# Macaron block (routed FFN, retention, routed FFN) on one core: two head groups' attention outputs in shared PSUM rows, and a GpSimd product and subtraction rewritten

## The chip, the cores and the metric

The kernel runs on 1 of the 8 cores of a Trainium2 chip. The metric is the device time of one execution in microseconds (us), as the median of several runs; lower is better. Engines: PE (TensorE, matmuls and transposes), DVE (VectorE), ACT (ScalarE), POOL (GpSimd), SP (issues DMAs). Each engine works through its own list of instructions in order, and waits on semaphores where the list says so.

## The reference, cut to what matters

```
x = x + 0.5 * ffn(layernorm(x));  x = x + retention(layernorm(x));  x = x + 0.5 * ffn(layernorm(x))     # x: (16, 256, 128)

def ffn(src):                                        # 16 heads of 8 dims, 4 experts, d_ff 512
    q, k, v = (src @ Wn + bn, split into 16 heads)
    probs = softmax(q @ k.T * 8 ** -0.5)
    x = layer_norm(src + (probs @ v) @ Wo + bo) * ln1_g + ln1_b
    keys = x @ router_w + router_b                   # one number a token
    e = remainder(floor(keys), 4)                    # each token to one of four experts
    return layer_norm(x + relu(x @ W1[e] + b1[e]) @ W2[e] + b2[e]) * ln2_g + ln2_b
```

## The kernel before, in words

There are three parts in a row: a phase of attention and experts for all 16 batches of 256 tokens, retention, and a second phase like the first. In an attention phase the step `i` of a software pipeline handles several batches at once: scores of batch `i`, softmax weights times values of batch `i-1`, output projection and first layer norm of `i-2`, routing and sorting of `i-3`, and preparation (layer norm, transposition) of `i+1` and `i+2`. A step has eight slots, `p = 0..7`, one for each pair of heads. In each slot PE runs a burst of eight matmuls (lines 576 and 582: scores of two heads of `i`, and the scores shifted by their maximum of two other heads), DVE takes the row maxima of the burst's first half (line 1357) and ACT the exponential of the second (line 1047). There is one pair of PSUM banks for each, so a burst waits for the maximum and the exponential of the slot before. All other work is placed by hand between the bursts, and the order of each engine's list is the order in the code. Steps `base+4` to `base+13` of a phase are a hardware loop, the others are written out.

PSUM banks beside these: `pv_bank` for weights times values, and `bank_a`, `bank_b`, `bank_c`, which many small steps use in turn; `take(which, reader, value)` waits until the last reader of the bank has finished.

What the change touches, by line:

- Values. ACT copies `v` to `v_nat` (line 1025). POOL's `place_v` (line 1849) spreads eight heads at a time into `v_st`, 32 columns a head: 8 values, a one (for the sum of the weights), zeros.
- `weigh_values(b, g)` (PE, line 632) multiplies group `g` (four heads) of `v_st` with the weights. Four heads fill 4 x 32 rows of `pv_bank`; the groups 0 and 1 lie side by side in columns, and groups 2 and 3 overwrite them after ACT's `out_pv` (line 1055) has copied all 512 columns to `att_un`.
- `att_to_tokens` (PE, line 641, slot 6) transposes the four groups for both halves of the tokens, eight 128x128 transposes into two banks. `normalize` (DVE, lines 1366 and 1368, in slot 6 for one half, in slot 7 for the other) takes reciprocals of the sums and multiplies.
- POOL's `rstd` and `normalise` (lines 1826, 1828, 1835): variance plus epsilon, power of -0.5, then for each half of the tokens `(x - mean) * rstd`. It is done for `prep` of batch `i+2` and for `ln1` of batch `i-2`. The result of `prep`, `s_nat`, is what PE transposes in slot 2 of the next step (line 545).
- POOL in a step, in this order: `place_v(i, 0)`; `rstd`, `normalise`, `make_x1` (lines 1854, 1856) and `own_row` (line 1867) of `i-2`; `place_v(i, 1)`; `sort_out` of `i-3` with two indirect DMAs (line 1879); `rstd`, `normalise` and `add_bo` (line 1840) of `i+2`.
- DVE's `route(b, base, n)`: `n = 0` is the product of `x1` with the router's weights (line 1403), `n = 1` its sum (line 1406), the rest tiny steps down to the expert's mask. The first three stand in slot 0 of step `i`, for batch `i-3`. `place` (lines 1425, 1429, 1431) in slots 4 and 5 turns masks into row numbers and counts.

Of the kernel before, what the change touches and what calls it, by code (L numbers as in the profile page):

```python
# [61 lines left out]
VC = 32  # L62

# [25 lines left out]
def spread_heads(a):  # L89


    return np.ascontiguousarray(a.reshape(2, RH // 2, RK, -1).transpose(1, 0, 2, 3)).reshape(QK_DIM, -1)

# [38 lines left out]
def packed(A):  # L132

    A = dict(A)
    columns = A.pop("W_qkv").T
    A["W_qkv"] = np.concatenate([spread_heads(columns[0:QK_DIM]), spread_heads(columns[QK_DIM:2 * QK_DIM]), columns[2 * QK_DIM:]], 0).T
    A["w_att"] = np.concatenate([A.pop(n) for n in ("Wq", "Wk", "Wv", "Wo")], 1)
    A["bias_rows"] = np.concatenate([A.pop("b1").reshape(CHUNKS, P), A.pop("bq")[None], A.pop("bk")[None], A["bv"][None]], 0)
    A["vecs"] = np.concatenate([A.pop(n).reshape(-1) for n in ("bv", "bo", "ln1_g", "ln1_b", "ln2_g", "ln2_b", "router_w", "router_b")])
    return A  # L140
# [9 lines left out]
def build(nc, A):  # L150

    ctx = ExitStack()
    with ctx:
# [40 lines left out]
        eps_ln = sb("eps_ln", [P, TT])  # L194
        eps_gn = sb("eps_gn", [P, 16])
# [12 lines left out]
        v_nat = sb("v_nat", [P, TT, P])  # L208
        v_st = sb("v_st", [P, TT, NH, VC])
        att_un = sb("att_un", [P, GROUPS, SEQ])  # L210
        rsum = sb("rsum", [P, TT * GROUPS, GH])
# [102 lines left out]
        seed = {"ln2": sem("seed_ln2")}  # L314
        ln_sem = {"prep": prep_ln, "ln1": ln1, "ln2": ln2}
# [212 lines left out]
        def _(pe):  # L528
# [114 lines left out]

            def att_to_dims(b, base):

                pe.wait_ge(att_ready, b * 2 + 2)
# [116 lines left out]
            def phase(base):  # L763
# [4 lines left out]
                def body(i, part=range(PAIRS)):  # L768
                    if live(i - 2, base):
                        turn["a"], turn["b"] = (att_ready, (i - 2) * 2 + 2), (att_ready, (i - 2) * 2 + 1)  # L770
# [1260 lines left out]
```

## Time and profile before

| | |
|---|---|
| median of 3 runs | 948.08 us (946.7 to 950.37) |
| the profiled execution | 951.38 us, its span 949.3 us |
| busy: PE, DVE, ACT, POOL | 87%, 80%, 70%, 60% of the span |
| first attention phase, its experts' tail | to about 310 us, to about 400 us |
| retention | about 400 to 570 us |
| second attention phase, its experts' tail | to about 850 us, to the end |

Times in the rows below are microseconds from the start of the span. Durations in one execution of the hardware loop repeat from step to step within some hundredths of a microsecond, so one step stands for all.

### The profile page before, as it was taken

The numbers are of one execution on the slowest core, as the hardware profiler recorded it, in microseconds if no ns is written. First come the engines' busy times: TensorE is split into PE (matmuls) and PEld (weight loads), VectorE is DVE, ScalarE is ACT, GpSimd is POOL, SyncE is SP. The second block draws the span as 40 slices with busy tenths as digits, with TensorE's granted clock in tenths as the row PEclk, the third lists the DMA queues.
The fourth block names the chain that finished last, engine by engine and source line by source line (L and its number), as shares of the span: only waits on it lengthen the run. The fifth ranks groups of instructions, "written<-read, shape, count | busy, mean of one in ns | idle before, by whom it ended". The sixth has DMA issues, their size and how long they took to land.

```text
span 949.3 us, 26557 instructions
## 1 busy us (share of the span) xinstructions
PE 828.5 (87%) x8607; PEld 625.8 (66%) x8607; DVE 762.0 (80%) x1935; ACT 665.3 (70%) x1370; POOL 568.6 (60%) x801
## 2 busy tenths in 40 slices
PE   4899899999999688479999979999999999996883
PEld 3566666666666688457877856666666666666883
DVE  5688788888897877669898864888888888978775
ACT  2588788888887477435454554988888888874774
POOL 5135667576665667627777682265765757565666
PEclk9999999999999999889999995999999999998998
DMA  9995698000004667230000000000000000046671
GB/s 288 380 417 82 164 412 362 12 11 22 11 23 134 187 197 236 76 87 2 0 0 0 1 1 2 2 13 12 11 22 11 22 11 11 24 143 201 193 240 48
DMA packets 41812, 96.64 MB, mean 102 GB/s; under 512 B 5224, under 2 KB 25470, under 8 KB 37260
## 3 DMA queue, kind: packets, MB, share of 16 engines
q1 hardware_dynamic: 36236, 83.11, 27.1%
q0 software_dynamic: 5504, 12.63, 3.8%
q8 instruction: 37, 0.61, 0.2%
q14 instruction: 35, 0.29, 0.1%
HBM read 43.64 MB, written 53.13 MB: 102 GB/s over the span
## 4 chain that ended last, share of the span: by engine, by line
PE 45%; DVE 20%; issue 18%; POOL 13%; DVEq 1%; ACT 1%; DMA 1%; POOLq 0%; ACTq 0%
DVE mx L1357 9%; PE duo L576 8%; PE duo L632 7%; PE duo L569 3%; POOL out L1930 3%; DVE qk_lo L1346 2%; PE duo L882 2%; POOL x_mid L1930 2%; PE duo L641 2%; PE duo L861 2%; POOL xs L1922 2%; PE duo L570 2%; PE duo L870 2%; PE duo L723 2%; PE duo L840 2%
## 5 line engine op out<-in xcount | busy, mean ns | idle before, releaser
L1357 DVE TENSOR_REDUCE mx<-duo 128x4 fp32r<-128x1024 f32 x256 | 312.2, 1220 | 73.5 <-PE duo L576 68.4
L1047 ACT ACTIVATE probs<-duo 128x1024 f32<-128x1024 f32 x256 | 263.3, 1029 | 58.3 <-PE duo L582 53.7
L576 PE MATMUL duo<-stacks 32*128 32x256 f32 x1024 | 133.6, 338 | 36.3 <-DVE mx L1357 27.3
L632 PE MATMUL duo<-probs,v_st 128*32 128x256 f32 x2048 | 140.3, 392 | 0.3
L582 PE MATMUL duo<-q_st,stacks 32*128 32x256 f32 x1024 | 131.5, 335 | 0.1
L576 PEld LDWEIGHTS duo<-stacks 32*128 32x128 f32 x1024 | 80.7, 191 | 72.6 <-issue 32.7
L1826 POOL TENSOR_TENSOR a_ln<-mv_ln,eps_ln 128x2 f32<-128x2 f32 x32 | 6.3, 197 | 145.3 <-DVE mv_ln L1322 145.1
L569 PE MATMUL duo<-qk_hi,sel_r 128*128 128x256 f32 x256 | 83.0, 345 | 7.6 <-DVE qk_lo L1346 7.6
L632 PEld LDWEIGHTS duo<-probs,v_st 128*32 128x32 f32 x2048 | 54.1, 110 | 41.5 <-issue 3.4
L723 PE MATMUL duo<-w,xs 128*128 x608 | 77.0, 281 | 4.3 <-DVE hidden L1524 1.8
L582 PEld LDWEIGHTS duo<-q_st,stacks 32*128 32x128 f32 x1024 | 77.9, 188 | 1.4 <-ACT probs L1047 0.5
L1879 POOL DMA_INDIRECT x_sorted<-rows,pos_all x64 | 66.2, 1035 | 19.8 <-issue 19.8
L723 PEld LDWEIGHTS duo<-w,xs 128*128 128x128 f32 x608 | 73.4, 197 | 5.5 <-issue 5.5
L1039 ACT ACTIVATE q_st<-duo 128x256 fp32r<-128x256 f32 x128 | 50.5, 395 | 35.0 <-PE duo L616 26.2
L570 PE MATMUL duo<-qk_lo,sel_r 128*128 128x256 f32 x256 | 69.6, 292 | 0.0
L1078 ACT ACTIVATE xs<-duo,wside 128x256 f32<-128x256 f32 x152 | 59.8, 471 | 10.7 <-PE duo L709 10.3
L569 PEld LDWEIGHTS duo<-qk_hi,sel_r 128*128 128x128 f32 x256 | 50.6, 198 | 23.8 <-DVE qk_lo L1346 12.5
L1033 ACT ACTIVATE stacks<-duo,small 128x256 fp32r<-128x256 f32 x128 | 61.9, 484 | 0.0
L1669 DVE TENSOR_TENSOR ret<-duo,dm 128x768 f32<-128x768 f32 x64 | 58.0, 947 | 1.2 <-PE duo L864 1.2
L1849 POOL TENSOR_TENSOR v_st<-v_nat,ones_wide 128x128 f32<-128x128 f32 x64 | 29.4, 461 | 44.4 <-PE duo L632 44.0
L1032 ACT ACTIVATE stacks<-duo 128x256 fp32r<-128x256 f32 x128 | 49.3, 385 | 8.6 <-PE duo L570 8.2
L1835 POOL TENSOR_SCALAR s_nat<-xs,mv_prep,rstd_prep 128x128 f32<-128x128 f32 x64 | 50.6, 795 | 6.5 <-POOL rstd_prep L1828 6.4
(219 smaller groups left out, 2178.8 us busy)
## 6 DMA issues: line engine op xcount, KB each, us to landing
x_sorted<-ret SPq DMA_DIRECT2D x2, 17476.0 KB, 49.0
wbuf<-w_pack SPq DMA_DIRECT2D x38, 512.0 KB
ret<-x_sorted SPq DMA_DIRECT2D x22, 257.0 KB
stacks<-x_sorted SPq DMA_DIRECT2D x12, 257.0 KB
wside<-w_pack SPq DMA_DIRECT2D x38, 66.0 KB
w_pack<-wbuf SPq DMA_DIRECT2D x2, 1024.0 KB, 8.4
decay_rows<-prow SPq DMA_DIRECT2D x1, 1536.0 KB
xs<-x_sorted SPq DMA_DIRECT2D x4, 257.0 KB
```

Of the source, the lines that this page charges most:

```text
L569: pe.matmul(half, sel_r[:, g, 2 * n, :], qk_hi[:, n, :], start=True, stop=False)
L570: last = pe.matmul(half, sel_r[:, g, 2 * n + 1, :], qk_lo[:, n, :], start=False, stop=True)
L576: return pe.matmul(score_bank[h % 2][:, t * SEQ:(t + 1) * SEQ], q_st[r:r + 32, g, t * P:(t + 1) * P], k_st[r:r + 32, g, :], start=True, st ...
L582: return pe.matmul(banks[h % 2][:, t * SEQ:(t + 1) * SEQ], k_st[r:r + 32, g, t * P:(t + 1) * P], q2_st[r:r + 32, g, :], start=True, stop=True)
L632: last = pe.matmul(pv_bank[32 * j:32 * j + 32, cols], v_st[:, t, h, :], probs[:, h % RING, t, :], start=(t == 0), stop=(t == TT - 1))
L723: last = pe.matmul(sum_bank(k)[:, t * P:(t + 1) * P], hid[:, n % 2, c, t * P:(t + 1) * P], w2[:, bass.ds(e * CPE + c, 1), :], start=(c == ...
L1033: act.activation(k_st[:, g, :], o[:, SEQ:2 * SEQ], ACT.Identity, bias=ones_col[:]).then_inc(ex_ready, 1)
L1047: act.activation(probs[:, h % RING:h % RING + 2, :, :], duo_now[:].rearrange("p (n t q) -> p n t q", n=2, t=TT), ACT.Exp, scale=SCALE).the ...
L1078: act.activation(hid[:, n % 2, c, :], bank[c][:, 0:SEQ], ACT.Relu, bias=wside[:, n % 3, c:c + 1]).then_inc(h_ready, 1)
L1357: dve.tensor_reduce(rows, score_duo[:].rearrange("p (n t k) -> p n t k", n=2, t=TT), AX.X, ALU.max, negate=True).then_inc(max_done, 1)
L1669: dve.tensor_tensor(ret[:, 2 * g:2 * g + 2, :], both, dm[:, 2 * g:2 * g + 2, :], ALU.mult).then_inc(ret_ready, 1)
L1879: pool.indirect_dma_start(x_sorted[b // BATCH], bass.IndirectOffsetOnAxis(pos_all[:, b - base, t:t + 1], 0), rows[:, b - base, t, :], None ...
```

## The change

Values of two groups go into one block of columns with an offset of 16, so that the output of the first group of a half lands in rows 0 to 8 and that of the second in rows 16 to 24 of each 32 rows, and both accumulate into the same 256 columns of `pv_bank`. So there is one copy of 256 columns for each half, four transposes in place of eight, into one bank, and one `normalize` in place of two, in slot 7. `Wo` and `bv` are put into the matching order on the host. The number of matmuls of line 632 stays. On POOL, `rstd` also computes minus the mean (one more small instruction), and `normalise` adds it in place of subtracting the mean. The product of the routing goes from DVE (slot 0 of step `i`, for `i-3`) to POOL (between `make_x1` and `own_row` of step `i`, for `i-2`), for all batches but the last of a phase.

```diff
+PAIR = GH * VC + VC // 2
...
-        v_nat = sb("v_nat", [P, TT, P])
-        v_st = sb("v_st", [P, TT, NH, VC])
+        v_nat = sb("v_nat", [P, 2, TT, P // 2])
+        v_st = sb("v_st", [P, 2, TT, 2 * PAIR])
...
                 if g == 0:
                     pe.wait_ge(va_ready, b + 1)
-                    wait(pe, un_ready, b * 2)
+                    wait(pe, un_ready, b * 2 - 1)
                 if g == 2:
                     pe.wait_ge(vb_ready, b + 1)
-                    pe.wait_ge(un_ready, b * 2 + 1)
-                cols = slice((g % 2) * SEQ, (g % 2 + 1) * SEQ)
+                    wait(pe, un_ready, b * 2)
+                half, second = g // 2, g % 2
+                into = pv_bank[:, half * SEQ:(half + 1) * SEQ]
                 for t in range(TT):
                     for j in range(GH):
-                        h = g * GH + j
-                        last = pe.matmul(pv_bank[32 * j:32 * j + 32, cols], v_st[:, t, h, :], probs[:, h % RING, t, :],
-                                         start=(t == 0), stop=(t == TT - 1))
+                        first = P * second + VC * j
+                        last = pe.matmul(into[32 * j:32 * j + 32, :], v_st[:, half, t, first:first + VC], probs[:, (g * GH + j) % RING, t, :],
+                                         start=(t == 0 and not second), stop=(t == TT - 1 and second == 1), skip_group_check=True)
...
-            def att_to_tokens(b, t):
+            def att_to_tokens(b):
                 pe.wait_ge(un_ready, b * 2 + 2)
-                o = take("ba"[t], att_ready, b * 2 + t + 1)
-                for g in range(GROUPS):
-                    last = pe.transpose(o[:, g * P:(g + 1) * P], att_un[:, g, t * P:(t + 1) * P], ident[:])
+                o = take("b", att_ready, b + 1)
+                for t in range(TT):
+                    for half in range(2):
+                        last = pe.transpose(o[:, (2 * t + half) * P:(2 * t + half + 1) * P], att_un[:, half, t * P:(t + 1) * P], ident[:])
                 last.then_inc(att_ps, 1)
...
-                act.activation(att_un[:, 2 * half:2 * half + 2, :], pv_bank[:].rearrange("p (a q) -> p a q", a=2),
-                               ACT.Copy).then_inc(un_ready, 1)
+                act.activation(att_un[:, half, :], pv_bank[:, half * SEQ:(half + 1) * SEQ], ACT.Copy).then_inc(un_ready, 1)
...
-            def normalize(b, t):
-                dve.wait_ge(att_ps, b * 2 + t + 1)
+            def normalize(b):
+                dve.wait_ge(att_ps, b + 1)
                 wait(dve, attT_ps, b)
-                m = (bank_b, bank_a)[t][:].rearrange("p (n c) -> p n c", c=32)
+                m = bank_b[:].rearrange("p (n c) -> p n c", c=VC // 2)
...
                         if p == 0:
                             if live(i - 3, base):
-                                for n in range(3):
+                                for n in range(0 if is_last(i - 3, base) else 1, 3):
                                     route(i - 3, base, n)
...
                 pool.wait_ge(done, b * 8 + 4)
                 pool.tensor_tensor(s["a"][:], s["mv"][:, :, 1], eps_ln[:], ALU.add).then_inc(done, 1)
+                if steps == 1:
+                    pool.tensor_tensor(s["c"][:], s["mv"][:, :, 0], minus_one[:], ALU.mult).then_inc(neg_mean[which], 1)
                 pool.wait_ge(done, b * 8 + 5)
                 pool.tensor_tensor(s["rstd"][:], s["a"][:], half_root[:, 0:TT], ALU.pow).then_inc(done, steps)
...
                 pool.wait_ge(done, b * 8 + 6)
+                pool.wait_ge(neg_mean[which], nth)
                 for t in range(TT):
-                    pool.tensor_scalar(dst(t), src(t), s["mv"][:, t, 0:1], s["rstd"][:, t:t + 1], ALU.subtract, ALU.mult).then_inc(done, 1)
+                    pool.tensor_scalar(dst(t), src(t), s["c"][:, t:t + 1], s["rstd"][:, t:t + 1], ALU.add, ALU.mult).then_inc(done, 1)
...
-                src = v_nat[:, :, 64 * half:64 * half + 64].rearrange("p t (h d) -> p t h d", h=8)
-                pool.tensor_tensor(v_st[:, :, heads, 0:HD], src, ones_wide[:].unsqueeze(1).to_broadcast([P, TT, 8, HD]), ALU.mult).then_inc((va_ready, vb_ready)[half], 1)
+                src = v_nat[:, half, :, :].rearrange("p t (a j d) -> p (t a) j d", a=2, j=GH)
+                pool.tensor_tensor(v_place(half, slice(0, HD)), src, ones_wide[:, 0:GH, :].unsqueeze(1).to_broadcast([P, 2 * TT, GH, HD]), ALU.mult).then_inc((va_ready, vb_ready)[half], 1)
...
+            def route_product(b, base):
+                pool.wait_ge(x1_ready, b * 2 + 2)
+                wait(pool, router, (b - 1) * 8 + 2)
+                pool.tensor_tensor(rprod[:].unsqueeze(1), x1_all[:, at(b, base), :, :],
+                                   rw_b.unsqueeze(1).unsqueeze(1).to_broadcast([P, 1, TT, P]), ALU.mult).then_inc(router, 1)
...
                         make_x1(i - 2, base)
+                        route_product(i - 2, base)
                         own_row(i - 2, base)
```

## Rows read from the trace of the kernel before

**Rows 1.** Page, busy time, share of the span and instructions of two engines.

```profile
PE 828.5 (87%) x8607; PEld 625.8 (66%) x8607; DVE 762.0 (80%) x1935; ACT 665.3 (70%) x1370; POOL 568.6 (60%) x801
```

**Rows 2.** Windows: stretch, its length, busy PE, PEld, DVE, ACT, POOL, clock, DMA.

```profile
210.00:260.00 50.00, 46.66 (x549) 32.20 (x548) 43.49 (x103) 42.71 (x81) 32.29 (x51) 1.00 0.04 16
700.00:750.00 50.00, 46.60 (x548) 32.50 (x544) 43.45 (x102) 42.64 (x81) 32.36 (x51) 1.00 0.04 16
```

**Rows 3.** The chain that ended last, one loop step: start, us, what.

```profile
706.72 0.41 DVE token_bufs L1403
...
719.02 0.87 PE duo L641 x8
...
723.63 0.41 DVE token_bufs L1403
```

**Rows 4.** Timeline of DVE in that step: start, us, [idle before, releaser].

```profile
707.76 1.22 DVE L1357 TENSOR_REDUCE mx<-duo 128x4 fp32r<-128x1024 f32 x1
...
718.22 0.15 DVE L1431 TENSOR_TENSOR counts<-counts,masks 128x8 bf16<-128x8 bf16 x1
...
718.44 1.19 DVE L1357 TENSOR_REDUCE mx<-duo 128x4 fp32r<-128x1024 f32 x1
...
721.51 0.25 DVE L1366 RECIPROCAL rsum<-duo 128x16 f32<-128x16 f32 x1
721.79 0.29 DVE L1368 TENSOR_TENSOR att_pair<-duo,rsum 128x128 f32<-128x128 f32 x1
722.49 1.23 DVE L1357 TENSOR_REDUCE mx<-duo 128x4 fp32r<-128x1024 f32 x1 [0.41 <-PE duo L576]
```

**Rows 5.** Timeline of ACT in that step.

```profile
705.79 1.02 ACT L1047 ACTIVATE probs<-duo 128x1024 f32<-128x1024 f32 x1 [0.45 <-PE duo L582]
...
707.86 1.05 ACT L1047 ACTIVATE probs<-duo 128x1024 f32<-128x1024 f32 x1
708.77 0.64 ACT L1055 ACTIVATE att_un<-duo 128x512 f32<-128x512 f32 x1
```

**Rows 6.** Timeline of PE in that step.

```profile
706.93 0.39 PE L576 MATMUL duo<-stacks 32*128 32x256 f32 x2 [0.15 <-ACT probs L1047]
...
709.22 0.39 PE L576 MATMUL duo<-stacks 32*128 32x256 f32 x2 [0.29 <-DVE mx L1357]
...
709.83 0.44 PE L545 MATMUL duo<-small,s_nat 128*128 128x128 f32 x2
...
711.12 0.39 PE L576 MATMUL duo<-stacks 32*128 32x256 f32 x2
...
719.83 0.38 PE L576 MATMUL duo<-stacks 32*128 32x256 f32 x2
```

**Rows 7.** Timeline of POOL in that step.

```profile
708.19 1.58 POOL L1835 TENSOR_SCALAR s_nat<-xs,mv_prep,rstd_prep 128x128 f32<-128x128 f32 x2 [0.21 <-POOL rstd_prep L1828]
...
715.66 0.20 POOL L1826 TENSOR_TENSOR a_ln<-mv_ln,eps_ln 128x2 f32<-128x2 f32 x1 [4.65 <-DVE mv_ln L1322]
...
718.49 0.74 POOL L1854 TENSOR_TENSOR token_bufs<-token_bufs,vecs_sb 128x256 f32<-128x256 f32 x1
```

**Rows 8.** Lines by form on POOL: busy, mean ns of one.

```profile
L1835 POOL TENSOR_SCALAR s_nat<-xs,mv_prep,rstd_prep 128x128 f32<-128x128 f32 x64 | 50.6, 795 | 6.5 <-POOL rstd_prep L1828 6.4
...
L1854 POOL TENSOR_TENSOR token_bufs<-token_bufs,vecs_sb 128x256 f32<-128x256 f32 x30 | 22.2, 739 | 2.5
...
L1809 POOL TENSOR_SCALAR vecs_sb<-vecs_sb 128x256 f32<-128x256 f32 x1 | 0.4, 444 | 1.6 <-DVE vecs_sb L1761 1.6
```

**Rows 9.** Timelines of DVE, then of POOL, behind the second attention phase.

```profile
841.64 0.16 DVE L1414 TENSOR_TENSOR rint<-rint 128x2 int32<-128x2 int32 x1
...
853.25 0.61 DVE L1414 TENSOR_TENSOR rint<-rint 128x2 int32<-128x2 int32 x1
...
853.10 1.33 POOL L1922 TENSOR_TENSOR xs<-ret,wside 128x256 f32<-128x256 f32 x2
```

**Rows 10.** The chain in the passage from retention to the second phase.

```profile
553.66 1.59 POOL s_nat L1835 x2
...
562.43 1.60 POOL s_nat L1835 x2
```

**Rows 11.** The chain behind the second attention phase.

```profile
849.42 0.45 PE duo L641 x4
...
851.30 0.34 DVE token_bufs L1403
```

More of the change, by code:

```diff
@@ L92, in spread_heads, with pair_heads @@
     return np.ascontiguousarray(a.reshape(2, RH // 2, RK, -1).transpose(1, 0, 2, 3)).reshape(QK_DIM, -1)
+def pair_heads(a):
+    return np.ascontiguousarray(a.reshape(2, 2, GH, HD, -1).transpose(0, 2, 1, 3, 4)).reshape(a.shape)
 def rotary_tables():
@@ L194, in build @@
         eps_ln = sb("eps_ln", [P, TT])
+        minus_one = sb("minus_one", [P, TT])
         eps_gn = sb("eps_gn", [P, 16])
@@ L314, in build @@
         seed = {"ln2": sem("seed_ln2")}
+        neg_mean = {"prep": sem("neg_mean_prep"), "ln1": sem("neg_mean_ln1")}
         ln_sem = {"prep": prep_ln, "ln1": ln1, "ln2": ln2}
@@ L769, in body @@
                     if live(i - 2, base):
-                        turn["a"], turn["b"] = (att_ready, (i - 2) * 2 + 2), (att_ready, (i - 2) * 2 + 1)
+                        turn["b"] = (att_ready, i - 1)
                     if live(i - 1, base):
-                        turn["c"] = (q2_ready, (i - 1) * 4 + 3)
+                        turn["a"], turn["c"] = (q2_ready, (i - 1) * 4 + 2), (q2_ready, (i - 1) * 4 + 3)
                     for p in part:
@@ L1024, in out_v @@
                 wait(act, vb_ready, b)
-                act.activation(v_nat[:], bank_b[:, 0:SEQ].rearrange("p (t d) -> p t d", t=TT), ACT.Copy).then_inc(v_ready, 1)
+                act.activation(v_nat[:].rearrange("p a t d -> p t a d"), bank_b[:, 0:SEQ].rearrange("p (t a d) -> p t a d", t=TT, a=2), ACT.Copy).then_inc(v_ready, 1)
             def out_expand(b, g):
@@ L1053, in out_pv @@
                 if half == 0:
-                    wait(act, att_ps, b * 2)
-                act.activation(att_un[:, 2 * half:2 * half + 2, :], pv_bank[:].rearrange("p (a q) -> p a q", a=2),
-                               ACT.Copy).then_inc(un_ready, 1)
+                    wait(act, att_ps, b)
+                act.activation(att_un[:, half, :], pv_bank[:, half * SEQ:(half + 1) * SEQ], ACT.Copy).then_inc(un_ready, 1)
             def out_attT(b, base):
@@ L1638, in body @@
                         elif p == 6:
-                            if live(i - 1, base):
-                                normalize(i - 1, 0)
                             if is_last(i - 2, base):
@@ L1644, in body @@
                             if live(i - 1, base):
-                                normalize(i - 1, 1)
+                                normalize(i - 1)
                         if isinstance(i, int) and base + 14 <= i <= base + 15:
@@ L1792, in _ @@
             pool.memset(eps_ln[:], LN_EPS)
+            pool.memset(minus_one[:], -1.0)
             pool.memset(eps_gn[:], GN_EPS * RV)
@@ L1795, in _, with v_place @@
             pool.wait_ge(set_pool, 1)
+            def v_place(half, cols):
+                blocks = v_st[:, half, :, :].rearrange("p t (a x) -> p (t a) x", a=2)
+                return blocks[:, :, 0:GH * VC].rearrange("p n (j c) -> p n j c", c=VC)[:, :, :, cols]
             def fills():
@@ L1799, in fills @@
                 pool.wait_ge(set_pool, 2)
-                for t in range(TT):
-                    last = pool.memset(v_st[:, t, :, HD:HD + 1], 1.0)
+                for half in range(2):
+                    last = pool.memset(v_place(half, slice(HD, HD + 1)), 1.0)
                 last.then_inc(set_pool, 1)
@@ L1826, in rstd, with normalise @@
                 pool.tensor_tensor(s["a"][:], s["mv"][:, :, 1], eps_ln[:], ALU.add).then_inc(done, 1)
+                if steps == 1:
+                    pool.tensor_tensor(s["c"][:], s["mv"][:, :, 0], minus_one[:], ALU.mult).then_inc(neg_mean[which], 1)
                 pool.wait_ge(done, b * 8 + 5)
                 pool.tensor_tensor(s["rstd"][:], s["a"][:], half_root[:, 0:TT], ALU.pow).then_inc(done, steps)
-            def normalise(b, which, src, dst):
+            def normalise(b, which, src, dst, nth):
                 s, done = ln_scratch[which], ln_sem[which]
                 pool.wait_ge(done, b * 8 + 6)
+                pool.wait_ge(neg_mean[which], nth)
                 for t in range(TT):
-                    pool.tensor_scalar(dst(t), src(t), s["mv"][:, t, 0:1], s["rstd"][:, t:t + 1], ALU.subtract, ALU.mult).then_inc(done, 1)
+                    pool.tensor_scalar(dst(t), src(t), s["c"][:, t:t + 1], s["rstd"][:, t:t + 1], ALU.add, ALU.mult).then_inc(done, 1)
             def add_bo(b, base):
@@ L1906, in body @@
                         wait(pool, resid_ready, i + 2)
-                        normalise(i + 2, "prep", lambda t: xs[:, i + 2 - base, t, :], lambda t: s_nat[:, t, :])
+                        normalise(i + 2, "prep", lambda t: xs[:, i + 2 - base, t, :], lambda t: s_nat[:, t, :], i + 3)
                         if i == -2:
```

22 lines of the change are left out of this document (10 added, 12 removed).

## The prediction

> **What bounds the kernel.** I read the page first. No engine is full [rows 1], so shares decide nothing. The windows say where to look: the loops of the two attention phases show the same picture, PE 46.6 of 50 us, DVE 43.5, and no DMA to speak of [rows 2]. Next the chain of waits for one step of the loop. It repeats: the router's product of DVE stands in it at 706.72 and again at 723.63, so a step takes 16.91 us [rows 3]. DVE's product and PE's eight transposes, which the change removes there, are both links of it. Last the timelines of the four engines in that step [rows 4 to 7], to see how much slack each link has against the other engines. The reader is to see there that almost none is free: the loop is a set of rings of nearly equal length.
>
> The inner ring is burst, maximum, burst. A second one matters more. POOL starts the layer norm of `i-2` when DVE delivers its moments (715.66, after 4.65 us of idling) and from there works without a pause until `s_nat` of `i+2` is ready at 708.19 + 1.58 = 709.77, in the next step [rows 7]. PE transposes it at 709.83 [rows 6], though its burst had begun at 709.22 and lasts some 0.43. PE goes from there in order to the burst of slot 3 (711.12), and on to the moments that POOL waits for. POOL's stretch is 709.77 + 16.91 - 715.66 = 11.0 us, the rest 5.9, together the whole step. POOL is 60% busy and yet a co-bound, with some 0.1 us of slack (up to 0.3 more, since DVE comes late to the maximum of slot 3 anyway).
>
> **The change, part by part.**
>
> *The product leaves DVE.* In slot 0 DVE is back to back, so the maximum of slot 1 starts 0.4 earlier if its burst is done; it began at 706.93, and ACT's exponential of the same burst starts at 707.86 at its own pace, behind four copies, and ends at 708.91 [rows 5]. The burst of slot 2 needs both. It came at 709.22, 0.24 behind the end of the maximum (707.76 + 1.22 = 708.98) [rows 4, 6]. PE's least distance behind an exponential is 706.93 - (705.79 + 1.02) = 0.12, so it can come at 708.91 + 0.12 = 709.03. Gain 0.19 a step of the 0.41 removed.
>
> *The product enters POOL.* Same shape as line 1854: 0.74 [rows 8], with some 0.1 for the wait on `x1_ready` before it. Queued behind it are `own_row`, `place_v(i, 1)`, both indirect DMAs of `i-3` and then all of `prep`: it adds 0.84 to POOL's stretch.
>
> *Minus the mean.* Two small instructions like line 1826, 0.20 each [rows 7]. The first falls partly into a wait of 0.07. Together 0.33. So POOL's stretch grows by 1.17, before the price of the addition.
>
> *Add for subtract.* This decides the case, and no row shows it. The present form takes 795 ns for 128 columns, four times a step [rows 8]. The only other instruction of that kind, line 1809, multiplies and adds on 256 columns and takes 444 ns. It has constants where the changed one has a column of scalars. So the bounds are: no change, 795, and for the cheap form between 222 (in proportion to columns) and 444 (columns free). 6.2 ns a column against 1.7 for one kind of instruction on one engine says that the price hangs on the operation or the operands; a two-operand instruction takes 739 for 256, 2.9 a column [rows 8]. A slow subtract explains it best, since reading a scalar once for each partition shouldn't cost by column. I take 330 ns, the middle of 222 and 444.
>
> The Trainium skill (GPSIMD Engine Reference, section 3.1) counts about 1.8 cycles of 1.2 GHz for each element of a tight one-input body, so by it line 1835 should already be near 0.2 us plus dispatch. The 795 ns of [rows 8] contradict that; if the page were right about the subtract there would be nothing to gain, and the sum would be that of the third case below.
>
> At 330, POOL's stretch changes by 1.17 - 4 x 0.465 = -0.69. It leaves the ring; PE finds `s_nat` ready.
>
> *Four transposes fewer.* 0.87 becomes 0.44 [rows 3]. The burst of slot 7 comes at 719.83, and the maximum it waits for ends at 718.44 + 1.19 = 719.63, plus the least distance 0.12 to 0.14: 719.77 [rows 4, 6]. So only 0.06 of 0.43 counts. Hidden by that maximum; without it, 0.43 would.
>
> *One `normalize`.* Two of 0.54 become one of about 0.70 (0.25 + 0.03 + 0.42, the last by the double of columns), all in slot 7, where it runs from 721.51 to 722.24, before the maximum at 722.49 that waits for PE [rows 4]. Worth nothing in the loop. The later release of `bank_b` (722.24) is before PE wants it, and `bank_a` no longer waits.
>
> *Half the copy.* ACT saves about 0.25 of 0.64, twice a step [rows 5]. What follows waits for PE. Nothing. `v` in a new order, `place_v` over other strides, and a second accumulation into the same columns: same counts and sizes, taken at nothing. If `place_v` cost 0.1 more, POOL's new slack would hide it.
>
> *A new collision.* DVE's step on counts (line 1431, 718.22) reads two operands in SBUF and stands before the maximum of slot 6, which is in the inner ring [rows 4]. An instruction of this type took 0.16 alone and 0.61 under a two-operand instruction of POOL [rows 9]; it seems held until POOL's ends. Now line 1835 lies over 718.22, and it does not hold DVE (0.15 [rows 4]). After the change line 1854 starts at 717.05 + 2x, with x the new price, and ends 0.73 later. For x = 0.33 that is 718.44: a hold of 0.10. For 0.444 it is 0.33; for 0.28 or less none.
>
> The Trainium skill (SBUF — State Buffer, section Who interferes with whom) says that a DVE instruction with two SBUF inputs is blocked by any GpSimd instruction that reads SBUF. By it line 1431 would be held already today, until 718.41; the 0.15 of [rows 4] disagrees for the one-input form, the 0.61 of [rows 9] agrees for the two-input form.
>
> *Outside the loop.* In the passage from retention POOL's chain holds two `prep` blocks [rows 10]: each 2 x 0.465 - 0.20 = 0.73 less, together 1.5. Behind each attention phase the chain runs over the transposes, `normalize` and the product [rows 11]: 0.43 + 0.38 + 0.41 = 1.2 each, 2.4 for two.
>
> **Sum.** Steps with routing: 3 to 15 of each phase, 26 in all. Each gains 0.19 + 0.06 - 0.10 = 0.15: 3.9 us. With 1.5 and 2.4: 7.8 us. The profiled execution took 951.38 (span 949.3, 2.1 around it), so its like would take 943.6; against the median of the runs, 948.08, it is 940.3.
>
> **Rivals.**
> 1. *The hold eats the gain* (ends within 0.5%). Cheap addition, but nearer 0.444 (scalars by pointer cost something). Hold 0.33, so each step loses 0.08: +2.1, passage -1.0, tails -2.4: -1.3, 946.8. For it: line 1431 lies just where line 1854 comes. Against: it needs a price in the upper part. Gain and loss cross at x = 0.40, and under 0.385 the sum is over 0.5%.
> 2. *The price stays at 795* (slower). POOL's stretch grows by 1.17 and is the ring; DVE's late maximum in slot 3 gives back up to 0.3. 0.83 to 1.17 a step x 26 = 22 to 30, passage +0.4, tails -2.4: 968 to 976, say 971. It decides from about x = 0.6: there POOL's ring equals today's step. For it: the scalars by pointer might be the dear part, which stay. Against: the 6.2 ns a column.
> 3. *ACT or PE take all of it*: the small gains of 0.19 and 0.06 vanish in waits that coincide, only passage and tails stay: -3.9, 944.2, within 0.5%.
>
> **Chances.** Forecast 0.57, rival 1 0.17, rival 2 0.18, rival 3 0.08. What a measurement can tell from no change is about 0.5%, 4.7 us. Faster 0.57, same 0.25, slower 0.18. The low end is x = 0.222 without hold (0.25 x 26 = 6.5, passage 1.9, tails 2.4, and holds in the tails avoided, up to 1.4 each): 13.6, 934.5. The high end takes in rivals 1 and 3 and some scatter: 951. Rival 2 is what is left out. The forecast's own range is 934 to 944.
>
> **What would show it.** Line 1835's successor near 330 ns, and no wait of PE for `s_nat` in the loop; the step at 16.76 us between two sums of the router; the burst of slot 2 at 0.19 less after that of slot 1; the counts step at about 0.25 in place of 0.15, with line 1854 above it; the product on POOL at 0.74; the four transposes followed at once by a wait for the maximum. The prediction is wrong if the addition costs over 400 ns, if DVE is held at other places by the longer row of two-operand instructions on POOL, or if placing values costs clearly more than 0.46.

## The result, and the profile after

| | before | after |
|---|---|---|
| median of the runs | 948.95 us (4 runs, 946.7 to 950.37) | 937.91 us (4 runs, 935.72 to 955.77) |
| the profiled execution, its span | 951.38, 949.3 us | 935.72, 933.9 us |

The ratio is 0.9878, 95% interval 0.9833 to 0.9922: faster by 1.2%. It leaves out the run of 955.77 us, which showed the lowest granted clock (0.957, the others 0.970 to 0.975). The forecast was 940.3 us, 934 to 951.

The page, busy time by engine: DVE 9 us less than before, PE 20 less, POOL 19 less, for a span that is 15.4 shorter [rows 1].

```profile
PE 808.0 (87%) x8479; PEld 605.3 (65%) x8479; DVE 752.7 (81%) x1841; ACT 656.9 (70%) x1370; POOL 549.9 (59%) x894
```

Lines by form on POOL: `normalise` takes 447 to 450 ns in place of 795 [rows 8].

```profile
L1851 POOL TENSOR_SCALAR s_nat<-xs,c_prep,rstd_prep 128x128 f32<-128x128 f32 x64 | 28.2, 447 | 8.4 <-POOL rstd_prep L1843 8.2
L1851 POOL TENSOR_SCALAR token_bufs<-token_bufs,c_ln,rstd_ln 128x128 f32<-128x128 f32 x60 | 26.4, 450 | 5.2 <-POOL rstd_ln L1843 5.1
```

One loop step after, timeline of DVE, answering to [rows 4]. The sum of the router (L1415) stands at 691.13 and again at 707.97: the step is 16.84 us, where it was 16.91 between two products [rows 3].

```profile
691.13 0.41 DVE L1415 TENSOR_REDUCE rkey<-token_bufs 128x2 f32<-128x256 f32 x1
...
702.34 0.33 DVE L1440 TENSOR_TENSOR counts<-counts,masks 128x8 bf16<-128x8 bf16 x1
...
702.75 1.19 DVE L1367 TENSOR_REDUCE mx<-duo 128x4 fp32r<-128x1024 f32 x1
704.71 1.23 DVE L1367 TENSOR_REDUCE mx<-duo 128x4 fp32r<-128x1024 f32 x1 [0.78 <-PE duo L586]
705.86 0.34 DVE L1375 RECIPROCAL rsum<-duo 128x32 f32<-128x32 f32 x1
706.24 0.42 DVE L1377 TENSOR_TENSOR att_pair<-duo,rsum 128x256 f32<-128x256 f32 x1
...
707.97 0.41 DVE L1415 TENSOR_REDUCE rkey<-token_bufs 128x2 f32<-128x256 f32 x1
```

The same step, PE: the bursts of slots 1, 2 and 7, the transposes of `s_nat` right behind the burst of slot 2, and four transposes in slot 6 in place of eight [rows 3, 6].

```profile
691.35 0.39 PE L586 MATMUL duo<-stacks 32*128 32x256 f32 x2 [0.16 <-DVE mx L1367]
...
693.35 0.39 PE L586 MATMUL duo<-stacks 32*128 32x256 f32 x2
...
693.79 0.44 PE L555 MATMUL duo<-small,s_nat 128*128 128x128 f32 x2
...
702.99 0.60 PE L653 MATMUL duo<-small,att_un 128*128 128x128 f32 x4
704.18 0.38 PE L586 MATMUL duo<-stacks 32*128 32x256 f32 x2 [0.59 <-DVE mx L1367]
```

And POOL [rows 7]: `s_nat` is ready at 693.32, before PE asks for it; the product (L1877) is new in the row.

```profile
692.44 0.88 POOL L1851 TENSOR_SCALAR s_nat<-xs,c_prep,rstd_prep 128x128 f32<-128x128 f32 x2 [0.27 <-POOL rstd_prep L1843]
...
701.92 0.73 POOL L1869 TENSOR_TENSOR token_bufs<-token_bufs,vecs_sb 128x256 f32<-128x256 f32 x1
702.73 0.73 POOL L1871 TENSOR_TENSOR rows<-token_bufs,vecs_sb 128x256 f32<-128x256 f32 x1
703.54 0.72 POOL L1877 TENSOR_TENSOR token_bufs<-rows,vecs_sb 128x256 f32<-128x256 f32 x1
```

The forecast's terms for one step can now be read off. From burst 1 to burst 2 it is now 2.00 us; it was 709.22 - 706.93 = 2.29 [rows 6]: 0.29 gained. The counts step takes 0.33 in place of 0.15, until the end of L1869 (702.65): 0.18 lost. The burst of slot 7 comes 704.18 - 703.94 = 0.24 behind the end of its maximum, although PE had long finished: the forecast had counted 0.12 to 0.14. Before, it came 719.83 - 719.63 = 0.20 behind [rows 4, 6], so 0.04 is lost here. Together 0.29 - 0.18 - 0.04 = 0.07, where the forecast had 0.15; all other distances between bursts are the same to 0.01.

A gain of 0.07 in each of 20 steps doesn't make 15.4 us. Most of that difference lies in two places outside the loops. The first is POOL ahead of its first indirect DMA, in the fifth step of the first phase. Before:

```profile
88.74 0.33 POOL L1862 TENSOR_TENSOR tick<-ones_wide 1x1 f32<-1x1 f32 x2
92.47 1.23 POOL L1879 DMA_INDIRECT x_sorted<-rows,pos_all  x1 [3.40 <-issue]
```

After:

```profile
85.50 0.33 POOL L1884 TENSOR_TENSOR tick<-ones_wide 1x1 f32<-1x1 f32 x2
86.01 1.22 POOL L1901 DMA_INDIRECT x_sorted<-rows,pos_all  x1 [0.19 <-issue]
```

POOL waited 3.40 us for nothing that this view shows; after, 0.19. That step took 21.67 us before and 16.71 after: 5.0 us. (Steps are counted here from the second `qk_lo` of DVE of one batch to that of the next.) The second place is the start of the second phase. Its first two steps took 20.07 and 19.63 before, 17.04 and 16.49 after: 6.2 us. The second step of the program adds 1.9 (21.77 before, 19.88 after). I had read none of these stretches.

### The profile page after: what moved, and what is told of

Same layout as the page of the kernel before. It is cut to its first block, busy times and chain, and to the rows that moved or that the text cites. A ratio compares the mean times of both kernels' runs of the same rounds, so it can differ in the third digit from the quotient of the medians.

```text
span 933.9 us, 26219 instructions
## 1 busy us (share of the span) xinstructions
PE 808.0 (87%) x8479; PEld 605.3 (65%) x8479; DVE 752.7 (81%) x1841; ACT 656.9 (70%) x1370; POOL 549.9 (59%) x894
## 4 chain that ended last, share of the span: by engine, by line
PE 48%; DVE 24%; issue 13%; POOL 7%; DMA 3%; SPq 1%; DVEq 1%; ACT 1%; POOLq 0%; ACTq 0%
DVE mx L1367 13%; PE duo L586 10%; PE duo L643 10%; DVE qk_lo L1356 3%; PE duo L893 2%; PE duo L735 2%; PE duo L579 2%; PE duo L624 2%; PE duo L872 2%; PE duo L881 2%; PE duo L851 2%; PE duo L854 1%; POOL x_mid L1953 1%; PE duo L930 1%; POOL out L1953 1%
## 5 line engine op out<-in xcount | busy, mean ns | idle before, releaser
L1367 DVE TENSOR_REDUCE mx<-duo 128x4 fp32r<-128x1024 f32 x256 | 312.2, 1219 | 71.2 <-PE duo L586 64.6
L579 PE MATMUL duo<-qk_hi,sel_r 128*128 128x256 f32 x256 | 81.0, 337 | 7.8 <-DVE qk_lo L1356 7.8
L624 PE MATMUL duo<-stacks,ident_r 128*128 128x256 f32 x128 | 52.3, 408 | 0.0
```

What stands on the lines that cost most here:

```text
L579: pe.matmul(half, sel_r[:, g, 2 * n, :], qk_hi[:, n, :], start=True, stop=False)
L624: pe.matmul(o[:, 0:SEQ], ident_r[:], q_st[:, g, :], start=True, stop=True)
L1367: dve.tensor_reduce(rows, score_duo[:].rearrange("p (n t k) -> p n t k", n=2, t=TT), AX.X, ALU.max, negate=True).then_inc(max_done, 1)
```

## Experiments

The kernels have their own line numbers. Steps are loop steps unless said otherwise, ratios are to the kernel before as timed alongside. A distance such as "6 to 7" is from the start of the burst of slot 6 to that of slot 7.

### The pause of POOL

**e1_fill**: the kernel before, and 20 one-element fills on POOL, once, ahead of the first indirect DMA.

```diff
+                            for n in range(20):
+                                pool.memset(filler[:, n:n + 1], 0.0)
```

> The kernel before with 20 tiny fills of one element on POOL at its start, where POOL idles, and nothing else. Theory A (POOL's pause of 3.4 us ahead of its first indirect DMA in step 3 is code that arrives late, at a place given by how many instructions stand before it): the pause goes away or moves, steps 3 and 4 are 4 to 5 us shorter, the whole 4 to 5 us below the kernel before. Theory B (the pause belongs to the data, to the clearing DMA or to the first use of the indirect DMA): it stays where it is, time as before within 0.3%.

The pause was gone, and the step took 17.17 us:

```profile
90.65 1.24 POOL L1880 DMA_INDIRECT x_sorted<-rows,pos_all  x1 [0.19 <-issue]
```

Ratio 0.993 [0.9881, 0.9978]. Twenty instructions that do nothing useful make the kernel before 0.7% faster.

The list of DMA transfers shows what the pause waits for. Queue 14 there is named "instruction" and moves packets of 8192 bytes. In the kernel before, one of its packets starts within the pause, at 90.45 us (DMA from 89 to 92.5 us):

```profile
q14 instruction: 1, 0.01, 0.6%
```

In e1_fill no packet of that queue moves between 61 and 100 us; the one before the pause's place had come at 60.07 (DMA from 59.9 to 60.5 us):

```profile
q14 instruction: 1, 0.01, 3.2%
```

In all five profiles with a pause the indirect DMA starts 2.01 to 2.02 us behind the start of such a packet (before, e10_before, e3_rows, e5_sub, e7_fill111); in the other nine the packet had come at 60 to 73 us. So POOL waits for its own instructions.

**e7_fill111**: the changed kernel, and 111 such fills at the same place.

```diff
+                            for n in range(111):
+                                pool.memset(filler[:, n:n + 1], 0.0)
```

> The changed kernel with 111 tiny fills on POOL at its start. The changed kernel has 17 more POOL records than the one before ahead of the first indirect DMA; 111 more make 128. Theory A (code arrives in pieces of 8192 bytes, which is 128 instructions of 64 bytes, and a piece ends there): the pause of some 3 us ahead of the first indirect DMA comes back, steps 3 and 4 take about 5 us more. Theory B (no period of 128): no pause there.

The pause came back, and the step was 21.7 us:

```profile
93.69 1.22 POOL L1902 DMA_INDIRECT x_sorted<-rows,pos_all  x1 [3.45 <-issue]
```

The packet of queue 14 starts inside the pause again, at 91.67; one more than in the other profiles, at 17.45, comes while the fills run. So the pause hangs on how many instructions POOL has had before this point, and not on what the change computes. That 17 more and 111 more bring it back fits a packet of 128 instructions; other numbers between 20 and 111 were not tried. 943.69 us median, ratio 0.9944 [0.9903, 0.9986]: with the pause put back, 5.3 us of the gain are left, about half. The fills are in this too: the first step took 19.96 in place of 18.69. The changed kernel against e1_fill, neither with the pause, gives much the same: 0.9878 / 0.993 = 0.9948, 4.9 us.

### The parts alone

**e2_add**: the kernel before with minus the mean and the addition, nothing else.

```diff
-pool.tensor_scalar(dst(t), src(t), s["mv"][:, t, 0:1], s["rstd"][:, t:t + 1], ALU.subtract, ALU.mult)
+pool.tensor_scalar(dst(t), src(t), s["c"][:, t:t + 1], s["rstd"][:, t:t + 1], ALU.add, ALU.mult)
```

> The kernel before with only the addition of minus the mean in place of the subtraction. Theory A (the forecast's accounts): POOL's layer norm takes 450 ns in place of 795 for each half, POOL leaves the ring, but the step of the loop doesn't get shorter, since DVE's product still fills slot 0, and DVE's counts now come under a two-operand instruction of POOL: 16.9 to 17.1 us a step, the loops 0 to +4 us, the passage from retention -1.0. Theory B (POOL's stretch alone set the step): the step falls by 0.2 or more, 16.7, 5 us in all. In both, the pause ahead of the first indirect DMA may be gone, since code on POOL moves: then 5 us less.

Steps of 17.03 to 17.48, one of 18.47 with a late signal of PE as in e4_dve below (16.88 before), ratio 1.002 [0.9975, 1.0065], although the pause was gone. The cheaper addition alone makes the loop slower: POOL's instructions come earlier and now lie over small steps of DVE, which are held until POOL's end, the first under the first half of `normalise` (702.28 to 702.7), the others under instructions of two operands. Timeline of DVE, one step:

```profile
702.42 0.33 DVE L1410 TENSOR_SCALAR rkey<-rkey,vecs_sb 128x2 f32<-128x2 f32 x1
703.79 0.21 DVE L1412 CAST rint<-rkey 128x2 int32<-128x2 f32 x1
704.04 0.38 DVE L1414 TENSOR_TENSOR rint<-rint,rkey 128x2 int32<-128x2 int32 x1
...
713.09 0.34 DVE L1433 TENSOR_TENSOR counts<-counts,masks 128x8 bf16<-128x8 bf16 x1
```

In the kernel before these took 0.23, 0.16, 0.17 and 0.15.

**e3_rows**: the shared rows alone (one copy of 256 columns a half, four transposes, one `normalize`), product and subtraction as before.

```diff
-                o = take("ba"[t], att_ready, b * 2 + t + 1)
-                for g in range(GROUPS):
-                    last = pe.transpose(o[:, g * P:(g + 1) * P], att_un[:, g, t * P:(t + 1) * P], ident[:])
+                o = take("b", att_ready, b + 1)
+                for t in range(TT):
+                    for half in range(2):
+                        last = pe.transpose(o[:, (2 * t + half) * P:(2 * t + half + 1) * P], att_un[:, half, t * P:(t + 1) * P], ident[:])
```

> The shared rows alone (half the transposes, copies and normalisations), POOL's arithmetic and the product as before. Theory A: 0.06 a step (16.85), 0.8 behind each phase, about 3 us in all, and the pause of POOL in step 3 stays, since POOL's code hasn't grown. Theory B (transposes on PE's path count in full): 0.43 a step, 16.5, 11 us in all.

Loop steps of 16.92 to 17.02: nothing gained, 0.05 lost, where 16.85 was expected. But in the second phase's steps 3 and 4, which are written out and have no counts step ahead of that maximum, the distance 6 to 7 falls from 2.28 and 2.29 (e10_before) to 2.00, and these steps take 15.53 and 16.08 in place of 15.81 and 16.55. The pause stays (3.59). Ratio 0.9982 [0.9929, 1.0036].

**e5_sub**: the changed kernel with the old subtraction (the diff of e2_add, reversed).

> The changed kernel with the subtraction as before (795 ns a half) and without the instruction for minus the mean. Theory A (POOL is a ring of its own, 0.84 longer by the product and with 0.1 to 0.4 us of slack): a step of 17.3 to 17.6 us, 12 to 19 us above the changed kernel. Theory B (POOL has slack, the price of the addition hardly counts): within 3 us of the changed kernel.

Steps of 17.31 to 17.5, as expected; ratio 1.0138 [1.0037, 1.024], by the two ratios some 25 us above the changed kernel, where 12 to 19 were expected. PE waits for `s_nat`, as rival 2 had it:

```profile
709.75 0.44 PE L553 MATMUL duo<-small,s_nat 128*128 128x128 f32 x2 [1.05 <-POOL s_nat L1845]
```

**e4_dve**: the changed kernel with the product back on DVE.

```diff
-                                for n in range(0 if is_last(i - 3, base) else 1, 3):
+                                for n in range(3):
...
-                        route_product(i - 2, base)
```

> The changed kernel with the product of the routing back on DVE. Theory A: slot 1 to 2 is 0.29 longer again, POOL's two-operand row is shorter; the step is 17.0 to 17.15 us, 3 to 7 us in all above the changed kernel. Theory B (the product on DVE was covered): as the changed kernel, 16.84 a step.

Steps of 18.45 to 18.56 but one, ratio 1.0288 [1.0195, 1.038]: far slower than expected. The chain of one step shows two losses. A piece of 0.99 stands where the second half of a burst takes 0.11 to 0.13 elsewhere, though its matmuls are recorded as ended at 715.58: PE's signal came 0.9 us late, and so in most steps. (Ends of matmuls in a profile are modelled, so it may be the matmul itself.)

```profile
715.08 0.39 PE duo L586 x2
715.47 0.99 PE duo L586 x2
...
716.59 0.08 DVE mx L1367
```

And DVE's step on two numbers is held under a two-operand instruction of POOL (0.23 elsewhere). Timelines of DVE and of POOL:

```profile
718.66 0.68 DVE L1417 TENSOR_SCALAR rkey<-rkey,vecs_sb 128x2 f32<-128x2 f32 x1
```

```profile
718.58 0.73 POOL L1856 TENSOR_TENSOR rows<-s_nat,vecs_sb 128x256 f32<-128x256 f32 x1
```

**e9_both** asks whether that is the product's price on DVE or a matter of where POOL's work lies: the product on DVE, and on POOL as well, into a buffer that nobody reads.

```diff
+                        spare_product(i - 2, base)
...
+                pool.tensor_tensor(spare[:].unsqueeze(1), x1_all[:, at(b, base), :, :],
+                                   rw_b.unsqueeze(1).unsqueeze(1).to_broadcast([P, 1, TT, P]), ALU.mult).then_inc(spare_done, 1)
```

> The changed kernel with the routing product back on DVE, as before, and the product on GpSimd kept as well, into a spare buffer that nothing reads. It tells why the run with the product back on DVE alone had steps of 18.46 us where 17.1 were expected. There the signal of the burst of slot 0 came 0.9 us behind its last matmul, once in each step, and another 0.45 went where a small step of DVE on two numbers (0.23 us elsewhere) took 0.68 beneath a product with two operands on GpSimd. Theory A (place in time): both depend on where GpSimd's work lies against DVE's, not on the product being on DVE. With GpSimd's row as long as in the changed kernel it lies where it does there, the late signal goes, and the step is 17.0 to 17.4. Theory B (the product on DVE by itself does it): the steps stay at 18.3 to 18.6. If only one of the two losses goes, the step is 17.5 to 18.1. A signal is called late if the maximum of slot 0 starts over 0.6 us behind the end of the burst that it reads.

Steps of 17.08 to 17.14, a few up to 17.41; no late signal at that burst, and L1419 back at 0.23. Theory A. With POOL's row the same, taking the product off DVE is worth 17.12 - 16.83 = 0.29 a step, and the distance 1 to 2 shows it: 2.28 against 2.00. A hold at another place costs nothing, for 2 to 3 is 1.90 with it and without:

```profile
699.41 0.41 DVE L1414 TENSOR_TENSOR token_bufs<-rows,vecs_sb 128x256 f32<-128x256 f32 x1
...
700.31 0.23 DVE L1419 TENSOR_SCALAR rkey<-rkey,vecs_sb 128x2 f32<-128x2 f32 x1
...
701.83 0.71 DVE L1423 TENSOR_TENSOR rint<-rint,rkey 128x2 int32<-128x2 int32 x1
```

One thing goes with the late signals, though no run tests it: in every loop step of e4_dve that has one, POOL starts an indirect DMA 0.04 to 0.19 us behind the first matmul of that burst. In e9_both and in the changed kernel a burst and an indirect DMA of POOL start so close only once (0.05 and 0.06), and there the signal is not late. So the closeness alone doesn't do it.

### The hold on the counts step

**e6_counts**: the changed kernel with that step behind the maximum of slot 6 in place of ahead of it.

```diff
-                                place(i - 3, base, 2)
...
+                            if live(i - 3, base):
+                                place(i - 3, base, 2)
```

> The changed kernel with DVE's step on counts moved from before the maximum of slot 6 to behind it. Theory A (the hold of that step under POOL's two-operand instruction cost 0.2 a step): the distance of the bursts of slots 6 and 7 falls from 2.45 to about 2.2, a step takes 16.6 us, 5 to 7 us in all less than the changed kernel. Theory B (the distance is set by the wake-up of PE alone): unchanged within 0.3%.

Steps of 16.56 to 16.64, and 2.20 from 6 to 7, so theory A. The step is now held for longer, where it stops nobody:

```profile
700.90 1.19 DVE L1367 TENSOR_REDUCE mx<-duo 128x4 fp32r<-128x1024 f32 x1
702.01 0.67 DVE L1440 TENSOR_TENSOR counts<-counts,masks 128x8 bf16<-128x8 bf16 x1
```

936.85 us median, ratio 0.9881 [0.9793, 0.9969]. **e12_counts** is the same kernel, timed beside the changed one:

> The changed kernel with DVE's counts step one slot later, behind the maximum, timed a second time, beside the changed kernel on the same chip. If the 0.24 us that its steps gained in the first profile are gained in every execution, 26 steps give 6 us, 0.65%: its median is 4 to 8 us below that of the changed kernel. The rival is that the gain of the loops is given back outside them (its first two steps of the second phase took 1.3 us more): then it is 1 to 3 us.

Median 938.95, ratio 0.983 [0.9767, 0.9892], against 944.48 and 0.9889 [0.9834, 0.9944] for the changed kernel (e11_after): 5.5 us less, the size that was expected, though the two intervals overlap. But it is not shown that the 26 steps gave it. In e12_counts' own profile they took 16.64 to 17.07 in the loops (a few signals of PE came 0.3 to 0.45 late), and all 26 only 1.6 us less than in e11_after; the two tails gave 5.4. In e6_counts' profile the 26 steps gave 5.6.

### The price of the addition

**e8_price**: the kernel before, with eight forms of the instruction run once.

```diff
+                            pool.tensor_scalar(probe[:, 0, 0:P], x[:, 0:P], m, r, ALU.subtract, ALU.mult)
+                            pool.tensor_scalar(probe[:, 2, 0:P], x[:, 0:P], m, r, ALU.add, ALU.mult)
+                            pool.tensor_scalar(probe[:, 4, 0:P], x[:, 0:P], 0.5, 0.25, ALU.mult, ALU.add)
+                            pool.tensor_scalar(probe[:, 6, 0:P], x[:, 0:P], 0.5, 0.25, ALU.subtract, ALU.mult)
```

> The kernel before with eight probes on POOL at its start, whose results nobody reads: x minus column times column on 128 and 256 columns, x plus column times column on 128 and 256, times and plus with constants on 128 and 256, minus and times with constants on 128, times and plus with columns on 128. If the subtraction is dear in itself: 795 and about 1400 to 1500 for the two subtractions, 795 with constants too. If the price of the cheap form hardly hangs on columns: 440 to 450 on both widths. If it is proportional: 220 to 330 on 128.

By form, in the order subtract with columns (256, 128), subtract with constants (128), add with columns (256, 128), constants without a subtract (256, 128):

```profile
L1917 POOL TENSOR_SCALAR probe<-vecs_sb,cols 128x256 f32<-128x256 f32 x1 | 1.2, 1219 | 0.0
...
L1916 POOL TENSOR_SCALAR probe<-vecs_sb,cols 128x128 f32<-128x128 f32 x1 | 0.8, 792 | 0.1
L1922 POOL TENSOR_SCALAR probe<-vecs_sb 128x128 f32<-128x128 f32 x1 | 0.6, 637 | 0.0
L1919 POOL TENSOR_SCALAR probe<-vecs_sb,cols 128x256 f32<-128x256 f32 x1 | 0.6, 550 | 0.0
...
L1918 POOL TENSOR_SCALAR probe<-vecs_sb,cols 128x128 f32<-128x128 f32 x1 | 0.4, 446 | 0.0
...
L1921 POOL TENSOR_SCALAR probe<-vecs_sb 128x256 f32<-128x256 f32 x1 | 0.4, 398 | 0.0
L1920 POOL TENSOR_SCALAR probe<-vecs_sb 128x128 f32<-128x128 f32 x1 | 0.3, 293 | 0.0
```

A subtract costs (1219 - 792) / 128 = 3.3 ns a column, an add (550 - 446) / 128 = 0.8. Scalars from a column in place of constants add 150 ns, whatever the width. The expectation missed twice: 1219 where 1400 to 1500 stood, and 637 with constants where 795 stood. Each form ran once here; the 446 is borne out by the 124 instructions of the changed kernel (447 and 450).

### What repeats from one execution to the next

**e10_before** and **e11_after** are the two kernels, unchanged, profiled again.

> The kernel before, unchanged, profiled a second time. The span of the first profile held three things outside the loops: a pause of 3.40 us of GpSimd ahead of its first indirect DMA, a step of 21.67 us there, and steps of 20.07 and 19.63 us at the start of the second attention phase with a granted clock of 0.50 to 0.69. Theory A: all three belong to the program (its place in the code and its own order of work), then the pause is 3.3 to 3.6 again, and the two steps are 20.1 and 19.6, both within 0.3. Theory B: the pause belongs to the program, the clock at the start of the second phase to the execution: then the pause is there, and the two steps come out elsewhere between 15.4 and 20. Theory C: both vary by execution. The steps of the loops are 16.88 to 16.93 by all of them.

> The changed kernel, unchanged, profiled and timed again, on the same chip as the next one. Pause ahead of the first indirect DMA 0.2, steps of the loops 16.80 to 16.92 by every theory. If the clock at the start of the second phase belongs to the program, the first two steps there are 17.04 and 16.49 again, within 0.3; if it belongs to the execution, they differ. Ratio to the kernel before 0.984 to 0.992.

Before: the pause is there again (3.56 us), the step 21.80; but the first two steps of the second phase took 16.27 and 15.42, not 20.07 and 19.63. Windows of that stretch (busy PE, PEld, DVE, ACT, POOL, then the granted clock), of the first execution and the second:

```profile
570.00:600.00 30.00, 28.26 (x208) 19.97 (x208) 15.82 (x22) 17.65 (x33) 4.71 (x10) 0.62 0.01 1
```

```profile
570.00:600.00 30.00, 25.66 (x277) 18.57 (x281) 22.10 (x35) 21.69 (x42) 10.66 (x16) 1.00 0.01 2
```

The granted clock was 0.62 over the first, so between its two levels of 1.2 and 2.4 GHz, and 1.00 over the second. After: 17.06 and 16.57, as in its first profile, pause 0.19, loop steps 16.73 to 16.89 and one of 17.12. Its span, however, was 943.0 against 933.9: 3.0 us more in the second step of the program, 3.3 between the phases, 2.4 behind the last. This scatter has nothing to do with the change, and is larger than most terms of the sum. It makes the first profiles poor witnesses for differences outside the loops. Theory B held for the kernel before; that the changed one repeated within 0.1, and e12_counts (18.28 and 16.57) with e6_counts (18.25 and 16.57), leaves open whether part of the clock goes with the program. The length of these steps goes with the clock granted in them: 16.27 and 15.42 us at 1.00 (e10_before, e8_price), 17.04 and 16.49 at 0.90 (after), 20.07 and 19.63 at 0.70 (before). In the second step of the program the clock was 1.00 in two profiles only, and those are the two short ones: 19.88 and 19.81 (after, e9_both), against 21.56 to 22.99 at 0.76 to 0.93 in the others.

## Why the prediction was right

The sign, the size (940.3 forecast, 937.91 measured) and the case (cheap addition, hold smaller than the gain) came out. But much of the agreement is luck: a pause worth 4.6 us that I had not seen stands in for the tails (2.4), which the profiles don't bear out, and for part of the passage. Without the pause the change is worth 5 us where 7.8 were forecast, and the interval of e7_fill111, 0.9903 to 0.9986, hardly tells the forecast (0.992) from rival 1 (0.9986). By the prediction's own sign, "wrong if the addition costs over 400 ns", its account of the price was wrong.

**Steps.** Forecast 3.9 us for 26. To keep the disturbed stretches out I compare the second profiles, steps 3 to 15 of each phase, with the fifth step taken from e1_fill. Phase 1: 32.84 + 17.17 + 152.02 + 16.50 = 218.53 before, 32.11 + 16.69 + 151.73 + 16.29 = 216.82 after. Phase 2: 218.07 and 216.15. Together 3.6 us. That this meets the 3.9 is luck: the loop steps gained 0.03 to 0.07 each, where 0.15 was forecast, the few written out around them 0.2 to 0.5 each. Those gain more in part because the shared rows count there: in steps 3 and 4 of the second phase the distance 6 to 7 fell from 2.28 and 2.29 to 2.00, and in e3_rows too, while in the loop it rose from 2.23 to 2.45.

**Product off DVE.** 0.19 forecast between bursts 1 and 2, 0.29 measured there, and 0.29 a step by e9_both. The forecast stopped at ACT's exponential, ending at 708.91. That one was itself behind the exponential of slot 0, which started 705.79 - 704.94 = 0.85 behind its burst; after the change it starts 706.77 - 706.19 = 0.58 behind, and the bound moves with it. Now PE goes from burst 1 to burst 2 without idling, so 2.00 is its own work.

**The new hold.** Forecast, with the place and the blocking instruction: 0.10. Measured 0.18, and e6_counts gave back 0.25. It was too small because the price was: 447 ns, not 330. By its own formula the hold at that price would be 0.33. (The formula is 0.03 too high: the step ends at 718.22 + 0.15 = 718.37, so 718.44 would be a hold of 0.07.) The rest is minus the mean: the 717.05 counts about 0.15 for it (718.49 - 2 x 0.795 = 716.90), and it cost nothing that the rows show. From POOL's first small instruction to L1869 it takes 701.92 - 699.79 = 2.13; before it took 718.49 - 715.66 = 2.83, and 2.83 less 2 x 0.348 is 2.13. So rival 1's price came true, and its sum (946.8) did not.

**POOL's stretch.** Forecast 0.69 shorter, measured 11.02 - 10.37 = 0.65 (699.79 to 693.32 + 16.84). Two errors cancel. The dearer addition takes back 4 x 0.117 = 0.47; the product and the two small instructions added 0.74, not 1.17, for the product came without the 0.1 of waiting (next start 0.68 later, 703.54 to 704.22), and the small ones fell into waits.

**Price of the addition.** The step that failed is the choice of 330 ns between 222 and 444. Its reason, that reading a scalar once for each partition shouldn't cost by column, was true and beside the point, since such scalars cost 150 ns in each instruction. The 444 ns of [rows 8] were taken as an upper bound; the true price lay just above it. The guess that the subtract is what costs by column was right.
The Trainium skill (GPSIMD Engine Reference, section 3.1) gives, beside the 1.8 cycles that the prediction drew on, 1.03 cycles for an element in the shortest bodies (its k up to 2, which I take for operations); at 1.2 GHz that is 0.86 ns, an estimate from the page's figures. The 0.8 ns a column of the add agrees with it, the 3.3 of the subtract is nearly four times that.

**Four transposes fewer.** 0.06 forecast. In the loop 0.04 was lost: PE now idles 0.59 and starts 0.24 behind the maximum, where it had started 0.12 to 0.14 behind when it came straight from work. [rows 4, 6] had shown this already: the burst at 709.22 came 0.24 behind its maximum, after 0.29 of idling. From burst 6 to burst 7 it takes 704.18 - 701.73 = 2.45, 0.22 more than before, the sum of this and the hold. e3_rows alone showed no gain in the loop either (16.92 to 17.02); in written-out steps it did, as said above.

**Passage.** One `prep` block on the chain was forecast 0.73 shorter. From its first instruction to the end of `add_bo` it is 3.58 us before (552.49 to 556.07) and 2.97 after (545.07 to 548.04): 0.61. In the span this drowns in 3 us of scatter.

**Tails.** Forecast 1.2 each. I had followed [rows 11], where PE's transposes and DVE's product set the time. After the change the chain there runs over POOL, and the product is a link of it again:

```profile
833.01 0.74 POOL rows L1871
...
833.84 0.72 POOL token_bufs L1877
834.55 0.66 POOL rows L1889
...
835.55 1.10 POOL x_sorted L1901
...
836.96 0.96 POOL x_sorted L1901
837.95 0.74 POOL xs L1945
838.74 0.04 issue
838.78 0.44 DVE hidden L1533
```

From the last `qk_lo` to this first `hidden` it took 35.66 to 35.68 us before (37.91 once, in e10_before's first phase), and 36.39, 36.43, 37.32 and 37.29 in the two profiles after, but 34.98 in e7_fill111; with the counts step moved, 34.57 and 34.59 in e12_counts, 34.54 and 35.97 in e6_counts. So the tail of the changed kernel can gain 0.7, and lost 0.7 to 1.6 in its own two profiles; part of it is again a late signal of PE (0.9 us at 831.23 in e11_after). Not settled.

**The rest.** The pause: 21.80 to 17.17 us by e1_fill, 4.6. With 3.6 for the steps that is 8.2 of the 11.0 us between the medians; the interval reaches down to 7.4. What is left, 2.8, is within the scatter of the first steps, the passage and the tails; no run assigns it.

## What to carry to other kernels

Moving work to another engine is paid for by where it then lies: on this kernel the same product on DVE cost 0.29 us a step, and 1.6 where POOL's row was one instruction shorter, and a cheaper instruction alone made the loop slower. Before you count a gain outside a loop, profile the same kernel twice, and look for idle time that the profile puts down to nothing, then at the instruction queues in the list of DMA transfers: one such pause was worth more than the whole change in the loops. Price an operation that no row shows by a probe of its own operands, not only of its width.

## What the runs showed of the hardware

- An instruction of two scalars on GpSimd, on 128 and 256 columns, costs 3.3 ns a column with a subtract in it and 0.8 with an add; scalars read from a column add 150 ns (e8_price).
- A pause of 3.4 to 3.6 us of GpSimd ahead of an indirect DMA comes and goes with the number of instructions before it: there in the kernel before (both profiles), e3_rows and e7_fill111, and 0.2 in nine profiles. In e5_sub it was 1.21, so it isn't all or nothing. In all five the indirect DMA starts 2.01 to 2.02 us behind the start of an 8192-byte packet of the queue named "instruction", which in the other nine came at 60 to 73 us.
- DVE's small instructions with two operands in SBUF are mostly held until a two-operand instruction of GpSimd ends (0.15 to 0.17 alone, up to 0.71 under one). Some with one operand are held too, also under a one-operand instruction of GpSimd: the cast L1419 at 693.03 of the changed kernel takes 0.32 in place of 0.16, until that of `s_nat` ends (693.32). The counts step was not held under the old subtraction (0.15 [rows 4]).
- A signal of PE can come 0.9 us behind the recorded end of its matmuls, step after step, at one place (e4_dve), and not at that place with GpSimd's work shifted by 0.7 us (e9_both). What holds it I don't know.
- In the loops PE starts 0.13 us behind a maximum when it has stood for less than 0.2 us, and 0.24 in most cases when it has stood for 0.28 or more (both kernels). It is no rule beyond them: outside the loops the same burst started 0.05 to 0.15 behind after up to 1.4 us of idling.
